# Attention over adjacency weights on one core: values of four key tiles at a time, and the keys of heads 2 and 3 made among the weights' products

## The reference

```python
c_adj = mean over channels of x                      # one number a node
A = |(|sigmoid(c_adj[m] - c_adj[n]) - 0.5|) - 0.5| * 2
Wg = adj * (A + A.T) / 2                             # 1024 x 1024
g = relu((x.T @ Wg) * para)                          # 256 x 1024
q = g.T, split into 4 heads of 64
k, v = split(x @ kv_w)                               # 4 heads of 64 each
attn = softmax(q @ k.T * scale)                      # 1024 x 1024 a head
x1 = layernorm(x + attn @ v)
```

## Time and profile before

| | us |
|---|---|
| median of 3 runs | 2922.38 (2921.91 to 2923.61) |
| the profiled execution | 2922.4 |
| its span in the trace | 2920.6 |
| PE busy | 2734.2 (94%) |
| DVE busy | 1979.5 (68%) |
| ACT busy | 1658.2 (57%) |
| POOL busy | 1280.7 (44%) |
| first layer, 16 batches | some 1993 of the span |

### The profile page before, as it was taken

How to read it: one execution, slowest core, us unless ns; L and a number is a source line. 1 busy time by engine, 2 the same in 40 slices (tenths; PEclk the granted TensorE clock), 3 DMA queues, 4 the chain that set the end, 5 groups by cost and what they waited for, 6 DMA issues and landing times. The chain is left out here.

```text
span 2920.6 us, 39408 instructions
## 1 busy us (share of the span) xinstructions
PE 2734.2 (94%) x12436; PEld 1848.1 (63%) x12436; DVE 1979.5 (68%) x2821; ACT 1658.2 (57%) x2148; POOL 1280.7 (44%) x700
## 2 busy tenths in 40 slices
PE   7999999999999999999999999996799999989953
PEld 5565665656656566565656656563688888868843
DVE  6787786877868778686877868773533433248877
ACT  6666576666667666576665757653422222237757
POOL 3755657565475755757566475645200000000034
PEclk9999999999999999999999999998899999999976
DMA  4123222232222232222232222221322232215547
GB/s 137 58 87 98 76 72 79 65 104 86 69 71 79 82 99 75 76 72 79 77 99 83 72 70 74 86 70 53 110 87 86 100 107 94 86 43 187 173 179 282
DMA packets 125646, 276.20 MB, mean 95 GB/s; under 512 B 12192, under 2 KB 62368, under 8 KB 119456
## 3 DMA queue, kind: packets, MB, share of 16 engines
q1 hardware_dynamic: 125600, 275.62, 29.6%
HBM read 178.79 MB, written 62.98 MB: 83 GB/s over the span
## 5 line engine op out<-in xcount | busy, mean ns | idle before, releaser
L304 POOL TENSOR_TENSOR psum<-psum,probs 128x1024 f32<-128x1024 f32 x320 | 784.1, 2450 | 149.4 <-ACT probs L372 130.1
L372 ACT ACTIVATE probs<-sc_ps 128x1024 f32<-128x1024 f32 x512 | 505.6, 1023 | 419.5 <-PE sc_ps L815 358.3
L544 DVE TENSOR_REDUCE mx<-mx_ps 128x1 f32<-128x512 f32 x768 | 521.5, 690 | 318.1 <-PE mx_ps L784 316.5
L831 PE MATMUL pv_ps<-probs,v 128*64 128x512 f32 x2048 | 492.4, 604 | 0.0
L815 PE MATMUL sc_ps<-qa,ka 128*128 128x512 f32 x1024 | 386.8, 403 | 0.0
L815 PE MATMUL sc_ps<-qb,kb 128*128 128x512 f32 x1024 | 380.9, 395 | 0.5
L784 PE MATMUL mx_ps<-ka,qa 128*128 128x512 f32 x768 | 316.5, 422 | 8.6 <-DVE mx L544 3.1
L831 PEld LDWEIGHTS pv_ps<-probs,v 128*64 128x64 f32 x2048 | 125.6, 136 | 224.6 <-issue 194.3
L815 PEld LDWEIGHTS sc_ps<-qa,ka 128*128 128x128 f32 x1024 | 187.5, 188 | 105.6 <-issue 64.1
L1170 DVE TENSOR_TENSOR agg_lo<-ag_ps,agg_hi 128x1024 fp32r<-128x1024 f32 x32 | 39.2, 1225 | 313.5 <-ACT agg_hi L1097 313.4
L784 PEld LDWEIGHTS mx_ps<-ka,qa 128*128 128x128 f32 x768 | 139.8, 187 | 173.3 <-issue 77.9
(11 more groups left out here) (180 smaller groups left out, 5552.8 us busy)
## 6 DMA issues: line engine op xcount, KB each, us to landing
adj_ring<-in_adj_dram SPq DMA_DIRECT2D x128, 512.0 KB, 3.7
pre_scratch<-pre SPq DMA_DIRECT2D x28, 1024.0 KB, 4.5
pre<-pre_scratch SPq DMA_DIRECT2D x28, 1024.0 KB, 4.9
x<-in_x_dram SPq DMA_DIRECT2D x16, 1024.0 KB, 5.6
kb<-ka SPq DMA_DIRECT2D x64, 256.0 KB, 3.4
qa<-qa SPq DMA_DIRECT2D x64, 256.0 KB, 3.1
res<-in_x_dram SPq DMA_DIRECT2D x16, 1024.0 KB, 5.6
x_scratch<-res SPq DMA_DIRECT2D x16, 1024.0 KB, 4.5
```

Source lines behind the costliest of these rows:

```text
L304: pool.tensor_tensor(psum[:, h % 2, :], probs[:, 0, :] if k == 1 else psum[:, h % 2, :], probs[:, k % PR, :], ALU.add).then_inc(s["pool_ad ...
L372: nc.scalar.activation(probs[:, i % PR, :], sc_ps[:, t % 2, :], ACT.Exp, scale=SCALE)\
L544: nc.vector.tensor_reduce(mx2[:, nh, n:n + 1], mx_ps[:, nh, :], AX.X, ALU.max)\
L831: ins = nc.tensor.matmul(pv_ps[nh * HD:(nh + 1) * HD, h % 2, :], v[:, i, h * HD:(h + 1) * HD], probs[:, i % PR, nh * BANK:(nh + 1) * BANK] ...
```

## The change

In words:

- **Groups of four.** PE makes the scores of four key tiles (two groups a head), then the values of the same four. `MAX_HALVES` is given for groups. `transpose_maxima` stands after the scores of group 1, `sum_up` of the head before after those of group 0, `transpose_sums` after those of group 1, and `transpose_back` at the end of the head, behind the last values. No values are left over for the next head.
- **Keys of heads 2 and 3.** `k_product(b, 1)` makes them in `mx_ps` after tile 1 of g, behind `sum_up`, which itself moves from inside tile 1 to its end. ACT and DVE split them between the weights of tiles 6 and 7.
- **After g**, one tile of v stands ahead of the first maxima of head 0, the others between them; the transposition of the maxima follows all of v. `v_copy(0)` moves ahead of `relu_q(1)` on ACT.
- **DVE**: `add_last(h-1)` stands ahead of all maxima of head h+1; row, inversion and `add_head(h-1)` behind all of them. In head 3, `xt_low(0)` moves ahead of `weigh(1)`, `w_low(2)` ahead of `invert_sums(2)`.
- **Head 3 on ACT**: `xt_high(0)` stands ahead of the exponentials, `tanh_half(3)` and the `k_high` of heads 0 and 1 behind the last two.
- **Head 3 on PE**: x of the next batch is transposed ahead of and after the scores of group 0, its keys of heads 0 and 1 are made after the scores of tile 5.

The diff, cut to its core:

```diff
-    MAX_HALVES = [[[0, 1, 1], [2, 1, 1, 1, 1], [2, 1, 1, 1, 1], [1, 1, 0, 0, 0]]] + \
-        2 * [[[0, 1, 1, 1, 1], [1, 1, 1, 1, 0], [2, 1, 1, 1, 1], [1, 1, 0, 0, 0]]]
-    SUM_PAIR, DEN_PAIR, BACK_PAIR = 1, 2, 3
+    MAX_HALVES = [[[3, 1, 1, 1, 1, 1], [2, 1, 1, 1, 1, 1, 1, 0]]] + 2 * [[[1] * 8, [2, 1, 1, 1, 1, 1, 1, 0]]]
+    GT = 4
...
                 w_high(b, 6)
+                k_high(b, 2)
+                k_high(b, 3)
                 w_high(b, 7)
                 q_high(b, 0)
                 q_high(b, 1)
                 relu_q(b, 0)
                 q_high(b, 2)
                 q_high(b, 3)
-                k_high(b, 2)
-                k_high(b, 3)
+                v_copy(b, 0)
                 relu_q(b, 1)
                 if not last:
-                    x_high(b + 1, range(0, 4))
-                v_copy(b, 0)
+                    x_high(b + 1, range(0, 6))
+                v_copy(b, 1)
                 if not last:
-                    x_high(b + 1, range(4, T))
-                v_copy(b, 1)
+                    x_high(b + 1, range(6, T))
                 for h in range(HEADS):
...
                 weigh(b, 6)
                 w_low(b, 5)
+                weigh(b, 7)
                 if before:
                     add_head(b - 1, HEADS - 1)
-                weigh(b, 7)
                 w_low(b, 6)
+                k_low(b, 2)
+                k_low(b, 3)
                 w_low(b, 7)
...
-                maxima(b, 0, range(0, 4))
-                k_low(b, 2)
-                maxima(b, 0, range(4, 5))
-                k_low(b, 3)
-                maxima(b, 0, range(5, T))
+                maxima(b, 0, range(T))
                 maxima_row(b, 0)
                 maxima(b, 1, range(T))
                 maxima_row(b, 1)
 
                 for h in (1, 2):
-                    maxima(b, h + 1, range(0, 1))
                     add_last(b, h - 1)
-                    maxima(b, h + 1, range(1, 4))
-                    maxima(b, h + 1, range(4, 7))
+                    maxima(b, h + 1, range(T))
+                    maxima_row(b, h + 1)
                     invert_sums(b, h - 1)
-                    maxima(b, h + 1, range(7, T))
-                    maxima_row(b, h + 1)
                     add_head(b, h - 1)
                     if h == 2 and not last:
                         weigh(b + 1, 0)
 
                 add_last(b, 2)
                 if not last:
+                    xt_low(b + 1, 0)
                     weigh(b + 1, 1)
-                    xt_low(b + 1, 0)
                     w_low(b + 1, 0)
                     xt_low(b + 1, 1)
                     weigh(b + 1, 2)
                     w_low(b + 1, 1)
+                    w_low(b + 1, 2)
                 invert_sums(b, 2)
                 if not last:
-                    w_low(b + 1, 2)
                     weigh(b + 1, 3)
                     k_low(b + 1, 0)
                     k_low(b + 1, 1)
...
-            def k_product(b):
-                wait(pe, s["xtl_done"], 2 * b + 2)
-                wait(pe, s["row_done"], 4 * b)
+            def k_product(b, c):
+                if c == 0:
+                    wait(pe, s["xtl_done"], 2 * b + 2)
+                    wait(pe, s["row_done"], 4 * b)
+                else:
+                    wait(pe, s["kl_done"], 4 * b + 2)
                 for nh in range(NH):
-                    ins = product(mx_ps[:, nh, :], k_terms(0, nh))
+                    ins = product(mx_ps[:, nh, :], k_terms(c, nh))
                 ins.then_inc(s["k_ready"], 1)
-
...
-                        if before and n == 1 and c == 0:
-                            sum_up(b - 1, HEADS - 1)
                     ins.then_inc(s["g_step"], 1)
+                    if before and n == 1:
+                        sum_up(b - 1, HEADS - 1)
+                    if n == 1:
+                        k_product(b, 1)
                     if before and n == 2:
...
             def body(b, last):
                 g_product(b)
-                k_piece(b, 0, 0)
-                k_piece(b, 0, 1)
+                v_product(b, 0, [0])
                 max_scores(b, 0, 0)
                 max_scores(b, 0, 1)
-                k_piece(b, 1, 0)
-                max_scores(b, 0, 2)
-                k_piece(b, 1, 1)
-                max_scores(b, 0, 3)
-                for m in range(4):
+                for m in range(1, 4):
                     v_product(b, 0, [m])
-                    max_scores(b, 0, 4 + m)
-                v_product(b, 1, [0, 1])
+                    max_scores(b, 0, m + 1)
+                max_scores(b, 0, 5)
+                v_product(b, 1, [0])
+                max_scores(b, 0, 6)
+                v_product(b, 1, [1])
+                max_scores(b, 0, 7)
+                v_product(b, 1, [2, 3])
                 transpose_maxima(b, 0)
-
-                v_product(b, 1, [2, 3])
                 scores(b, 0, 0, [0])
                 scores(b, 0, 1, [0])
                 for h in range(HEADS):
                     more = h + 1 < HEADS
                     halves = iter(range(NH * T))
 
-                    def maxes(p, k):
-                        for j in itertools.islice(halves, MAX_HALVES[h][p][k] if more else 0):
+                    def maxes(g, k):
+                        for j in itertools.islice(halves, MAX_HALVES[h][g][k] if more else 0):
                             max_scores(b, h + 1, j // NH, [j % NH])
 
-                    for p in range(PAIRS):
-                        i = 2 * p
-                        if p == 0:
-                            units = [(n, [0], range(NH)) for n in (i, i + 1) if h]
-                            units += [(n, [1], range(NH)) for n in (i, i + 1)]
-                        else:
-                            units = [(n, (0, 1), [nh]) for n in (i, i + 1) for nh in range(NH)]
+                    for g in range(T // GT):
+                        group = range(GT * g, GT * (g + 1))
+                        units = [(n, (0, 1), [nh]) for n in group for nh in range(NH)]
+                        if g == 0 and h == 0:
+                            units[0:2 * NH] = [(n, [1], range(NH)) for n in (0, 1)]
+                        elif g == 0:
+                            units[0:NH] = [(0, [part], range(NH)) for part in (0, 1)]
+                        if (h, g) == (3, 0) and not last:
+                            transpose_x(b + 1, 0)
                         for k, (n, parts, part_halves) in enumerate(units):
-                            maxes(p, k)
+                            maxes(g, k)
                             scores(b, h, n, parts, part_halves)
-                        maxes(p, len(units))
-                        if h and p == DEN_PAIR:
+                            if (h, g, k) == (3, 1, 2 * NH - 1) and not last:
+                                k_product(b + 1, 0)
+                        if (h, g) == (3, 0) and not last:
+                            transpose_x(b + 1, 1)
+                        if more and g == 1:
+                            transpose_maxima(b, h + 1)
+                        if h and g == 0:
+                            sum_up(b, h - 1)
+                        if h and g == 1:
                             transpose_sums(b, h - 1)
-                        if more and p == PAIRS - 1:
-                            transpose_maxima(b, h + 1)
-                        if h and p == BACK_PAIR:
-                            transpose_back(b, h - 1)
-                        if not last:
-                            prepare(b + 1, h, p)
-                        if h and p == SUM_PAIR:
-                            sum_up(b, h - 1)
-                        if p:
-                            values(b, h, i - 2)
-                            values(b, h, i - 1)
-                        elif h:
-                            values(b, h - 1, T - 2)
-                            values(b, h - 1, T - 1)
-                values(b, HEADS - 1, T - 2)
-                values(b, HEADS - 1, T - 1)
+                        for i in group:
+                            values(b, h, i)
+                    if h:
+                        transpose_back(b, h - 1)
```

More of the change, by code:

```diff
@@ L342, in k_high @@
                 wait(act, s["k_ready"], 2 * b + h // 2 + 1)
-                src = (mx_ps, pv_ps)[h // 2]
-                nc.scalar.activation(ka[h][own(h), :], src[own(h), :, :].rearrange("p a n -> p (a n)"), ACT.Copy)\
+                nc.scalar.activation(ka[h][own(h), :], mx_ps[own(h), :, :].rearrange("p a n -> p (a n)"), ACT.Copy)\
                     .then_inc(s["kh_done"], 1)
@@ L410, in prepare @@
                 if (h, p) == (3, 0):
-                    xt_high(b, 0)
                     w_high(b, 0)
@@ L418, in prepare @@
                     distance(b, 3)
+                if (h, p) == (3, 3):
                     tanh_half(b, 3)
@@ L446, in body @@
                 q_high(b, 3)
-                k_high(b, 2)
-                k_high(b, 3)
+                v_copy(b, 0)
                 relu_q(b, 1)
```

(38 more changed lines are left out.)

8 lines of the change are left out of this document (removed).

## The result

| | before | after |
|---|---|---|
| median, us | 2922.48 (2921.91 to 2923.61) | 3181.45 (3178.47 to 3187.72) |
| the profiled execution | 2922.4 | 3187.7 |
| mean granted clock | 0.976 | 0.912 |

A forecast was written before the change was run, and what follows sets the result against it. The matrix engine (PE) was taken as the bound, a batch costing its stream plus its waits; a saving of 2.5 us against added waits gave +5.6 us a batch, together +87, so 3009 us, range 2950 to 3055.

The forecast's parts named there:

- sixteen values in a row: PE's values of a group of four key tiles: sixteen instructions in a row take 3.58 us.
- wait at the start of head 2: PE waits for DVE's first maximum, behind transpose_back, add_head and add_last: +2.05 us a batch.
- at the start of head 1: PE waits for maxima behind add_last, which waits for POOL's sixth addition: +0.9 us a batch, bounds 0 and 2.
- `sum_up` in g: PE reaches sum_up at 28.4, DVE is ready at 30.6: a wait of 2.2 us against 1.06, +1.1 a batch.
- PE leaves head 3: End of head 3 on PE, put at 22.8 us, with transpose_back 1.0 us later through DVE and POOL collisions.
- The wait of q: Before the first maxima of head 0, q_times_para starts 0.25 us before g ends: wait 1.45 against 0.1, +1.3 a batch.
- Head 3: Waits for an exponential and xt_low(1), and six DVE and POOL collisions in place of about four: +1.55 us a batch.
- The saving of the groups: Values groups fall from 15 to 8 a batch at about 0.36 us each: 2.5 us a batch saved.
- The clock: Rival: PE's clock falls after two waits a batch, 1.8 us each, 58 us on top: 3067 us, chance 0.05.
- DVE did not catch up: Rival: at the start of heads 1 and 2 DVE catches up, only the saving is left: 2882 us, chance 0.12.
- The debt paid once: Rival: waits at heads 1 and 2 stay, those of 1.0, 1.1 and 1.3 us fall away: 2958 us, chance 0.22.
- The group's price: Rival: every pair of values pays 0.36 us, grouped or not, so 40 us come back: 3049 us, chance 0.06.

The follow-up runs named there:

- the keys alone: Kernel before with the keys of heads 2 and 3 in g and the changed order after g, pairs of key tiles kept: 3050.9 us, ratio 1.0442.
- the last run above: Kernel before with sum_up behind tile 1 of g and both k_low behind the row of head 0: 2909.0 us, ratio 0.9953.
- the groups-only run: Kernel before with groups of four and changed head 3, but transpositions kept inside the head and add_last behind two tiles of maxima: 2938.7 us, ratio 1.0056.
- the run with 14 spare ones: Changed kernel with 14 spare full matmuls behind the first two maxima of head 0: 3116.0 us, ratio 1.0664.
- the two runs of the repaired heads: Changed kernel with the order at the ends of heads 1 and 2 undone, groups of four kept: 3053.0 us (3030.9 to 3075.0), ratio 1.0443.

## Why the prediction was wrong

**Direction and place: right.** Nearly every wait is where the steps put it. DVE at the start of head 2:

```profile
812.54 1.63 DVE L578 SCALAR_TENSOR_TENSOR res<-pv_ps,rden,res 128x64 f32<-128x64 f32 x8 [4.05 <-PE pv_ps L844]
814.08 1.22 DVE L560 TENSOR_TENSOR psum<-psum,probs 128x1024 f32<-128x1024 f32 x1
815.21 1.97 DVE L543 TENSOR_REDUCE mx<-mx_ps 128x1 f32<-128x512 f32 x3
```

| step | forecast | in the trace |
|---|---|---|
| sixteen values in a row | 3.58 | 3.59 (776.56 to 780.15) |
| wait at the start of head 2 | 2.05 | 2.16 |
| at the start of head 1 | 0.9 | 1.13 |
| `sum_up` in g | 2.2 | 2.11 |
| first maxima of head 0 | 1.45 | 2.09 |
| PE leaves head 3 | 22.8 | 21.81 |
| whole order at full clock, 16 batches | +87 us | +99 us |

**The wait of q, ahead of the first maxima of head 0, +0.64.** The step counted 0.5 us of waits on ACT between `add_last` and `moments`. It missed a wait for PE. `invert_sums`, queued on DVE between the weights of two tiles, needs the transposed sums. PE makes them behind tile 2 of g, and `k_product` now stands ahead of that tile:

```profile
731.00 0.21 DVE L566 RECIPROCAL rden<-pv_ps 128x8 f32<-128x8 f32 x1 [2.58 <-PE pv_ps L836]
...
745.42 2.35 DVE L530 TENSOR_TENSOR scr<-sc_ps,neg_para 128x1024 f32<-128x1024 f32 x2
```

From there DVE takes 14.4 us to `q_times_para` and PE 13.9 to the end of g, so `q_times_para` starts 0.51 after the end of g (744.91) and not 0.25 before it. The same slip made the expectation for the keys alone too small: there `invert_sums` waits 0.95, and `q_times_para` starts 0.52 after g. In the last run above, which moves `sum_up` but not the keys, `invert_sums` doesn't wait, so it is the keys' place that does it.

**Head 3, 1.0 too much.** POOL and DVE got in each other's way less than counted: the chain from `add_head` (693.45) to the weights of g (722.67) is 29.2 us and not 30.4, and the second `invert_sums` held up the transposition by about 0.2. PE and DVE were both a microsecond early, so the wait in g came out right: two misses that cancel. That +87 is so near +99 is luck of the same kind, since misses either way stand in the sum.

**The saving of the groups.** Head 1 runs at the full clock in both traces. It lasts 21.96; less its wait of 1.13, and 0.24 that the transposition of the maxima waits (it starts 0.47 after a matmul of 0.23), that is 20.6 against 21.07: 0.5 saved by two groups fewer, where 2 x 0.36 was forecast; the groups-only run shows still less, 0.7 of busy time a batch for seven groups.

**The clock: the step that failed.** The sum has no term for it; it was taken as granted in full. It was a rival, at 3067 us with a chance of 0.05. What spoke against it was the row of a wait of 1.06 with the clock at 1.00, and that the new waits are "little over 2 us in a busy engine"; no row of before had a wait of 2 us in a batch, so nothing bore that second half. The runs show the fall behind 40 of the changed kernel's 46 such waits (14 of 15 in the maxima, 12 of 15 in g, 14 of 16 in head 2). Its price was too small as well: 1.8 us a wait is right for g and head 2 (half of 3.4 us is 1.7), where full matmuls follow; in the maxima it is about 9 us, because the matmuls there didn't bring the clock back. And there were three such waits, since that of q came out at 2.09. With 158 us for the clock the forecast of the order, 3009, would have read 3167. The Trainium skill (TensorE: Matmul & The Clock Gate, section Why this matters for your kernels) advises against idle gaps of more than about 3 us between bursts of matmuls; here the clock fell behind gaps of 2.1, so the measurement decides against reading that figure as a safe bound.

**The other rivals.** DVE did not catch up: its first maximum of head 2 starts at 815.21, 3.05 after the head, not within 0.8. The debt paid once: none of the waits in g and at q fell away. The group's price: the sixteen are as forecast, but the saving isn't. Between 0.7 and 1.8 us a batch (seven times 0.25) came of 2.5, so this rival was right in part.

## What to carry to other kernels

Count an idle gap of TensorE twice: once as the time it lasts, and once as what the lower clock may cost behind it, 1.7 us where full matmuls followed and about 9 where small ones did. With small matmuls behind them (64 rows, or 256 columns) even waits of 0.9 us cost 36 us where they lasted 14 in all, and with waits of 2.1 us spare full matmuls, in the gap or behind it, were cheaper than idling. And when a step moves on one engine, follow every instruction queued behind the one that waits for it: the wait of `invert_sums` for PE, 0.95 us where only the keys moved, made the wait ahead of the first maxima 2.1 where 1.2 had been expected, and that is the one that cost most.

## What the runs showed of the hardware

- In the changed kernel the clock fell behind 40 of 46 waits of some 2.1 us. Ahead of the first maxima of head 0 it fell behind waits of 0.9, 1.2 and 1.8 us in 4, 6 and 4 of 15 batches, and behind 2.9 us in all. It never fell behind 1.13 in head 1 of the changed kernel, nor behind 1.06 in g before, but four times behind 0.81 in the groups-only run. Why one batch falls and the next doesn't behind the same wait (1.17 in both batches shown) wasn't settled, nor why only 11 of 31 waits of some 2.1 us are followed by a fall once the wait of q is filled.
- PE busy 5.00 of 5.00 us doesn't mean that the clock is back: with 64-row and 256-column matmuls a stretch at 1.2 GHz lasted 17 to 24 us, with full 128x512 ones 3.4 us, or 6.8 in some batches of the run with 14 spare ones.
- One kernel's time can differ from run to run with them: the two runs of the repaired heads differ by 44 us, at mean granted clocks of 0.922 and 0.940. There is a trace of the slower one only, so the falls of the other aren't counted.
